# A PSUM bank released by ScalarE's copies instead of GpSimd's sum, and three products of a token mixer at earlier points

## The reference

```python
h = _L0_tok_ref(x, ...)                    # token mixer, then a convolution over time
h = h + _L0_attn_ref(_layernorm(h), ...)   # 8 heads of 64, softmax, position scores
h = h + _L0_ffn_ref(_layernorm(h), ...)    # 8 experts, 2 per token, and a shared one
h = h + _L1_attn_ref(_layernorm(h), ...)   # linear attention (no softmax)
h = h + _L1_ffn_ref(_layernorm(h), ...)    # 64 experts, 8 per token, 256 slots each

def _L0_tok_ref(x, Wl, bl, bias, Wc, bc, W2, b2):
    # K = 31, H = 4: each token has 4 x 31 weights of its own over its neighbours
    logits = (x @ Wl.T + bl).reshape(Bq, Tq, H, K)
    w = jax.nn.softmax(jnp.where(valid, logits, -jnp.inf), axis=-1)
    y = einsum('bthk,btkhd->bthd', w, xg).transpose + bias
    z = conv1d(y, Wc) + bc                 # 128 -> 512 channels, 31 taps: 345 tokens are left
    return selu(z) @ W2.T + b2

def _L0_ffn_ref(x, gate_w, w1, w2, sg_gate, sg_up, sg_down):
    topk_w, idx = jax.lax.top_k(xf @ gate_w.T, 2)      # softmax over the two -> comb
    h = silu(einsum('td,ehd->teh', xf, w1))
    eo = einsum('teh,edh->ted', h, w2)
    routed = einsum('te,ted->td', comb, eo)            # the sum over experts e
    shared = silu(xf @ sg_gate.T) * (xf @ sg_up.T) @ sg_down.T
    return routed + shared
```

## Time and profile before

| | |
|---|---|
| time, median of 3 runs | 2265.41 us (2263.96 to 2266.24) |
| the profiled execution | 2269.88 us |
| its span | 2268.1 us |
| TensorE busy | 1861.0 us, 82% |
| VectorE busy | 1404.4 us, 62% |
| ScalarE busy | 977.4 us, 43% |
| GpSimd busy | 866.4 us, 38% |
| iteration 8 (even) | 1040.49 to 1146.53 us |
| iteration 9 (odd) | 1146.53 to 1258.69 us |
| iteration 15 (the last full one) | 1775.70 to 1879.00 us |

### The profile page before, as it was taken

How to read it: one execution, slowest core, us unless ns; L and a number is a source line. 1 busy time by engine, 2 the same in 40 slices (tenths; PEclk the granted TensorE clock), 3 DMA queues, 4 the chain that set the end, 5 groups by cost and what they waited for, 6 DMA issues and landing times.

```text
span 2268.1 us, 47779 instructions
## 1 busy us (share of the span) xinstructions
PE 1861.0 (82%) x17168; PEld 1501.3 (66%) x17168; DVE 1404.4 (62%) x4603; ACT 977.4 (43%) x2557; POOL 866.4 (38%) x750
## 2 busy tenths in 40 slices
PE   3688999999999999999998999999978777166660
PEld 2576777877777787878786878787755555144430
DVE  4784465767667766767676766666665757344440
ACT  2353454545454636454645454544535441021110
POOL 1000011113343425251524262434334356768885
PEclk9999999999999999999999999999989898577775
DMA  6773754534344333433342423233200001067765
GB/s 210 270 255 119 264 170 140 168 114 118 109 124 140 109 104 116 125 91 118 92 145 58 138 79 124 64 119 98 79 5 7 7 4 26 8 121 120 117 89 73
DMA packets 167562, 251.52 MB, mean 111 GB/s; under 512 B 67362, under 2 KB 122981, under 8 KB 166577
## 3 DMA queue, kind: packets, MB, share of 16 engines
q10 hardware_dynamic: 43656, 153.58, 21.1%
q0 software_dynamic: 56672, 51.14, 10.5%
q1 hardware_dynamic: 67016, 43.91, 7.4%
HBM read 203.03 MB, written 87.40 MB: 128 GB/s over the span
## 4 chain that ended last, share of the span: by engine, by line
PE 43%; issue 21%; POOL 12%; DMA 9%; DVE 7%; ACT 5%; ACTq 1%; POOLq 0%; SPq 0%; DVEq 0%
PE W L1038 17%; PE Cb L1038 17%; POOL slots_dram L952 8%; DMA odd_sum_dram<-qv 5%; PE L L1038 4%; PE W L1211 3%; DMA out<-qv 3%; POOL h L945 2%; PE L L1066 1%; ACT xh L1539 1%; POOL odd_sum_dram L1018 1%; DMA ring<-filters_dram 1%; DMA band<-band_dram 1%; ACT conv_s L1504 1%; ACT seq_hi L1466 1%
## 5 line engine op out<-in xcount | busy, mean ns | idle before, releaser
L1038 PE MATMUL Cb<-seq_hi,ring 128*128 128x174 f16 x4356 | 572.8, 240 | 20.6 <-DVE seq_lo L1769 10.4
L1038 PE MATMUL Cb<-seq_lo,ring 128*128 128x174 f16 x2178 | 506.5, 240 | 0.0
L952 POOL DMA_INDIRECT slots_dram<-rows,slot_i x384 | 457.4, 1191 | 111.0 <-issue 111.0
L1038 PEld LDWEIGHTS Cb<-seq_hi,ring 128*128 128x128 f16 x4356 | 386.6, 98 | 51.9 <-DVE seq_lo L1769 11.1
L945 POOL TENSOR_TENSOR h<-h,xh 115x384 f32<-115x384 f32 x120 | 120.1, 1001 | 707.1 <-ACT xh L1539 706.9
L1583 ACT ACTIVATE area_k<-W 115x345 f32<-115x345 f32 x384 | 176.5, 460 | 331.7 <-PE W L1211 316.9
L2007 DVE SCALAR_TENSOR_TENSOR area_h<-area_h,W 128x345 f32<-128x345 f32 x256 | 131.4, 514 | 236.6 <-ACT area_h L1529 207.4
L2100 DVE CUSTOM_DVE_ANT_0 area_h<-W,offsets 115x345 f32<-115x345 f32 x384 | 196.4, 513 | 113.3 <-PE W L1038 103.5
L1038 PE MATMUL W<-area_k,qv 64*115 64x345 f16 (+1 forms) x1920 | 253.4, 381 | 14.8 <-POOL h L945 8.8
L1211 PE MATMUL W<-ident,area_h 115*115 115x115 f32 x1152 | 197.3, 281 | 72.5 <-POOL h L945 51.2
L1577 ACT ACTIVATE area_h<-area_h,nmax 115x345 f32<-115x345 f32 x384 | 224.8, 585 | 31.0 <-DVE nmax L2100 30.5
(11 more groups left out here) (270 smaller groups left out, 3069.0 us busy)
## 6 DMA issues: line engine op xcount, KB each, us to landing
ring<-filters_dram ACTq DMA_DIRECT2D x252, 512.0 KB
slots_dram<-in_empty_slots POOLq DMA_DIRECT2D x8, 1544.0 KB, 14.6
area_k<-slots_dram SPq DMA_DIRECT2D x64, 193.0 KB
filters_dram<-ring ACTq DMA_DIRECT2D x24, 512.0 KB, 4.4
band<-band_dram SPq DMA_DIRECT2D x64, 189.0 KB
filters_dram<-offsets ACTq DMA_DIRECT2D x12, 512.0 KB, 4.3
slots_dram<-rows,slot_i POOLq DMA_INDIRECT x384
x_win<-in_xpad SPq DMA_DIRECT2D x16, 252.0 KB
```

Of the source, the lines that this page charges most:

```text
L952: pool.indirect_dma_start(out=slots_d, out_offset=bass.IndirectOffsetOnAxis(ap=slot_i[parity(b)][:, m:m + 1], axis=0), in_=rows[parity(b)] ...
L1038: return pe.matmul(o, l, r, start=start, stop=stop)
```

## The change

Two edits. First, `wait_freed` waits for `y_scaled` instead of `y_added` where the bank's previous use is the product of one of the eight routed experts, and either that use was in the iteration before or the iteration isn't the last one. The shared expert's product (Y8) keeps `y_added`. Second, three entries of `MIX_AT`: products 5, 6 and 7 go from the points 9, 11 and 13 to 8, 10 and 11.

```diff
-MIX_AT = {r: n for n, r in enumerate([1, 2, 4, 5, 7, 9, 11, 13])}
+MIX_AT = {r: n for n, r in enumerate([1, 2, 4, 5, 7, 8, 10, 11])}
@@
 FREED |= {("Y", e): ("y_added", e + 1, 1) for e in range(E0 + 1)}
+SCALED = [("Y", e) for e in range(E0)]
@@ def wait_freed(eng, ro, use):
             name, k, behind = FREED[prev]
+            if prev in SCALED and (ago or ro.kind != "last"):
+                name = "y_scaled"
             sig = named[name]
             eng.wait_ge(sig.h, sig.at(back(ro.b, ago + behind), k))
```

## The result

The changed kernel takes 2223.52 us (median of 4 runs, 2222.60 to 2225.58), the kernel before 2264.68 (4 runs, 2263.17 to 2266.24): 41.2 us less, ratio 0.9819, 95% interval 0.9802 to 0.9836. The forecast was 2218, with a range of 2207 to 2240. The profiled execution fell from 2269.88 to 2225.58 us, by 44.3; the first of these two lies 5.2 us above its kernel's median, the second 2.1 above.

A forecast was written before the change was run, and what follows sets the result against it. The prediction took TensorE, busy 1861.0 of 2268.1 us, as the bound. Earlier bank release 41, the mixer's products 0 and clock 9, less 3 for unseen releases, made 47 us: 2218 us, range 2207 to 2240.

The forecast's parts named there:

- Bank waits, steady part: Experts' banks in steady iterations, free after ScalarE's copies instead of GpSimd's sum: 33.7 of 39.9 us come back, before deductions.
- the tails: Tail of the matmul before each of 60 waits, left out of listed gaps: 0.03 us each, 1.6 us added.
- Nothing from T16 in odd iterations: Transposes behind expert 5, iterations 1 to 11: earlier start only lengthens the next wait for the exponential; 6.5 us don't come.
- Iterations 14 and 15: Waits for GpSimd's sum there, 20.0 us in 14: 13.8 come back; three or four of six slow-clock stretches go.
- the rival that had 3%: VectorE work released sooner by TensorE is blocked until GpSimd's sum ends, 1 us in each of 60 waits: 2265; 3%.
- The clock: TensorE's 1.2 GHz stretches behind shrinking waits: five or six of 13 go, 1.7 us each, 9 us; bounds 0 and 22.
- The mixer: Products 5, 6, 7 at points 8, 10, 11: 6.1 us gained before the logits, 6 lost in gaps behind band transposes.
- Part two: Moving products 5, 6, 7 to earlier points: net gain 0, bounds a gain of 6 and a loss of 2.4 us.
- The band of tile 3: Its read wanted 0.45 us sooner, 7.3 us left: no cost; as a rival, it comes late, 2277, 3%.
- The waits for `xh`: Sign in the profile after: waits for ScalarE's scaling replace those for the sum, some 6 us steady, 6 in iterations 14 and 15.
- the 24 new waits for `area_b`: Sign in the profile after: TensorE waits of 0.1 to 0.4 us each, 24 of them, from the products' new points.
- The rival of other waits: TensorE comes 1 us sooner but the exponential or VectorE's maximum doesn't: half of the 41, no clock, 2241; 15%.

The follow-up runs named there:

- bank waits alone: Changed kernel's earlier bank release with products 5, 6, 7 at old points 9, 11, 13, against the kernel before: 2221.01 us (0.9822), on another chip 2239.95 (0.9850).
- experiment 3: Changed kernel, but transposes behind expert 5 in odd iterations with a next pair wait for GpSimd's sum again: 2233.63 us, against 2235.72 for the changed kernel.
- experiment 2: ScalarE's `seq_hi` and VectorE's `seq_lo` work moved later: in the changed kernel 2206.66 us (0.9759), in the kernel before 2261.20 us (0.9995).
- experiment 5: Mixer's points varied on top of the earlier bank release: old points 2239.95 us against 2234.94 for the changed kernel; with later `seq_hi`, product 7 at 12: 2225.75.
- later `seq_hi` copies: Changed kernel with ScalarE's `seq_hi` copies three steps later in odd iterations, `seq_lo` behind them: 2206.66 us (0.9759), on another chip 2228.04 (0.9804).
- group 1: Four kernels run on one chip beside the kernel before (2261.7 us): bank waits alone, mixer alone, changed kernel and kernel before each with later `seq_hi` copies.
- group 3: Four kernels run on one chip beside the kernel before (2273.1 us): bank waits alone, changed kernel, later `seq_hi` copies, and those with product 7 at 12.

## Why the prediction was right, and where its terms were off

The direction and the place were right, and the measured 41.2 us lie 6 under the forecast's 47. Of these 6, 3 are the choice of the execution: the sum was worked out on the profiled one, and between profiled executions the fall is 44.3. This one splits into 33.7 us of idle time in iterations 1 to 15 (26.7 + 7.0), 12.3 of busy time (0.7 + 11.6), less the 1.7 by which iteration 1 starts later. The forecast had 38 of waits and 9 of clock. So its total is in part luck: too much for the waits of iterations 14 and 15, and too little for the clock and for the mixer. By its steps:

- **Bank waits, steady part: right.** 33.7 less 6.5 and 0.5, with 1 us added for the tails, was 28 us for iterations 1 to 13. The bank waits alone gave 1404.4 - 1374.8 = 29.6 us against the trace of before and 25.4 against the trace of their own group. That 0.14 us lie between ScalarE's copies and TensorE's start, as with the sum, held to the hundredth (1205.95 to 1206.09).
- **Nothing from T16 in odd iterations: right.** The second wait is 1.46 us, 1.4 was forecast, and experiment 3 shows it at no cost.
- **Iterations 14 and 15: the sum right, the split wrong, by luck.** 12.7 us of waits and some 6 of clock were forecast, 18.7; measured are 18.6, but 7.0 of idle time and 11.6 of busy time. What is missing of the waits is the rival that had 3%: VectorE is held by GpSimd. In iteration 15, of the changed kernel:

```profile
1782.26 1.16 POOL L957 DMA_INDIRECT slots_dram<-rows,slot_i  x1 [0.30 <-issue]
...
1782.75 2.31 DVE L1850 TENSOR_SCALAR rows<-h,mv,rstd 115x128 f32<-115x128 f32 x3
...
1783.45 1.00 POOL L950 TENSOR_TENSOR h<-h,xh 115x384 f32<-115x384 f32 x1
...
1785.11 0.42 PE L1182 MATMUL L<-ident,rows 115*128 115x115 f32 x2 [1.43 <-DVE rows L1850]
...
1803.94 1.92 DVE L1943 TENSOR_TENSOR ss<-ss,gpen 115x192 f32<-115x192 f32 x1
...
1804.62 1.01 POOL L950 TENSOR_TENSOR h<-h,xh 115x384 f32<-115x384 f32 x1
...
1806.46 0.37 PE L1043 MATMUL W<-w2eT,area_h 128*115 128x128 f32 x1 [1.38 <-DVE area_h L2012]
```

  The first of the three `rows` instructions took 1.79 us, where the shortest takes 0.33, and ended at 1784.54, 0.09 behind the sum. L1943 took 1.92 us, where it took 0.36 in all its 16 places of before, and ended 0.23 behind the sum; L2012, for which TensorE then waits 1.38, starts only behind it. Iteration 14 has the same two (1.42 and 1.34 us). All eleven traces with the new bank waits show the four, with waits of TensorE of 1.32 to 1.44 us, and none of the three with the old ones does. Together the four waits are 5.6 us, and 5.7 of the forecast's are missing; two old waits of 1.06 for a row maximum went for them, so the match isn't exact. With the old waits the same instructions ran at another moment against GpSimd's. Both VectorE instructions began beside a scatter, and whether the scatter or the sum behind it held them these runs don't separate.
- **The clock: too small.** 9 us were forecast, and busy time fell by 12.3. Half the length of all stretches at 1.2 GHz in iterations 1 to 15, as an estimate of what they cost, is 37.5 us before (those behind waits that the change doesn't touch among them) and 21.9 after: 15.7, of them 12.5 in iterations 14 and 15. I had counted only the stretches that began right behind a wait for the sum or the logits, and of the six of them in iterations 14 and 15 had let three or four go. All six went, and the one at 1776.6 too; two of 10.2 us that stand behind other waits stayed. That those behind expert 5 in odd iterations stay was nearly right: there were five (I had counted six), four stayed, and one of them lasts twice as long; experiment 2 shows what they hang on.
- **The mixer: mis-sized.** "I take 6, between the two. Part two then gives 6.1 - 6 = 0": it gave 5.0 us (experiment 5), 4.1 by itself. The gaps in front of products 5 and 7 are 0.12 us in the trace and not 0.21 (0.05 and not 0.14 behind seven matmuls), and both together cost 0.28 or 0.35 us an iteration, under 4 us in all; the gain before the logits is 1.44 in an odd iteration and not 1.03. Its bounds, from a gain of 6 to a loss of 2.4, held. The band of tile 3 made nobody wait.
- **What wasn't in the sum** is ScalarE's late copy: 10 times 0.64 to 1.06 us in the trace of the changed kernel, 7.9 us together. The trace of before has no such stall over 0.43 us, but smaller ones of 0.3 to 0.4 behind transposes 9 and 15 of even iterations. Whether the larger ones come with the chip or the change makes them out of the small ones stays open, and so does what they cost. Iterations 8 and 9 took 104.8 and 110.6 us where 103.5 and 109.5 were forecast, and 15 took 93.3 where 94 was. The waits for `xh` were to be 6 us in the steady part and 6 in iterations 14 and 15 and are 3.8 and 5.7; the 24 new waits for `area_b` don't show in the list, being 0.05 to 0.12 us each.
- **VectorE held by the sum, in the steady iterations.** L1941 beside the sum again took 0.93 us and ended at 1207.06, 0.03 behind it, as the Trainium skill's page "SBUF — State Buffer" (section "SBUF: two separate sides") has it for a two-port VectorE operation that starts second. There it cost TensorE little: the row maxima, which read PSUM, took 0.485 to 0.534 us (0.491 to 0.542 before), with the sum beside 75 of them (77 before), and the waits of the transposes for them are 14.0 us in iterations 1 to 13, 14.1 before; those for `area_h` L2012 rose from 5.0 to 6.4. With the later `seq_hi` copies it did cost something, the 0.83 us of experiment 2.

The rival of other waits says "Half of the 41 and no clock: 2265.4 - 24 = 2241"; half of the 41 is 20.5, so its own case is 2245.

## What to carry to other kernels

A buffer is free with its last reader, not with the end of the chain that its data go down: look in the list of waits for an engine that waits for one which never touched the buffer. What such a wait gives back is its length up to the difference of the two signals, less what the next wait on the same engine takes. Work queued in the wrong place (here 2.1 us of copies) can cost nothing before such a change and 7 to 10 us after it. And look at what the engines that are let go sooner will run beside: here VectorE instructions met GpSimd's and held TensorE up by 1.3 to 1.4 us in four places. Two ratios are compared only if both were measured on one chip.

## What the runs showed of the hardware

- Chips differ by more than a run does: the kernel before took 2261.7, 2270.5 and 2273.1 us on three, each at one time, and the whole change had the ratios 0.9853, 0.9834 and, in the result, 0.9819. The slower two have ScalarE's stalls in all their traces (12 to 15 each), the fastest has none; the changed kernel's trace in the result has ten.
- VectorE instructions on SBUF were held beside GpSimd's work: a 115x128 TENSOR_SCALAR took 1.79 us (0.33 at the shortest) and a 115x192 TENSOR_TENSOR 1.92 (0.36), each begun beside a scatter and ended 0.09 and 0.23 us behind the sum that follows it. Those that read PSUM, L2105, stayed within 0.485 to 0.534 us.
- Short idle times of TensorE cost twice where its clock falls behind them: on the chip of group 1 the later `seq_hi` copies took all stretches at 1.2 GHz out of iterations 1 to 13, and busy time there fell from 1318.4 us (bank waits alone) to 1309.5 for the same matmuls. On the chip of group 3, where ScalarE's stalls leave idle times of their own, four such stretches stayed; three of them begin 1.9 to 3.0 us behind such a late copy.
